# One run of row sums and value products per unit in a fused cross-attention kernel, with sums in a tile of their own and four input tile slots

## The chip, the cores and the metric

One core of a Trainium2 chip. The metric is the time of one execution in device microseconds. Engines: PE is TensorE's matmul, PEld its weight load, DVE is VectorE, ACT is ScalarE, POOL is GpSimd, SP issues transfers. Each engine runs its own instructions in the order written and waits on semaphores.

## What is computed

Cross-attention with 32 batches of 512 queries and 512 keys, width 512, 16 heads of 32, all in float32:

```python
qn, kvn = layer_norm(q, q_norm_g, q_norm_b), layer_norm(kv, kv_norm_g, kv_norm_b)
Q, K, V = heads(qn @ Wq), heads(kvn @ Wk), heads(kvn @ Wv)
attn = softmax(einsum('bhqd,bhkd->bhqk', Q, K) / sqrt(D_HEAD), axis=-1)
ctx = einsum('bhqk,bhkd->bhqd', attn, V)
out = q + gelu(ctx @ Wo + bo)        # exact gelu
```

## The kernel before

**Units and steps.** A batch is four steps, and step s works on several units at once. A unit is four heads of a batch: there are four in a batch, 128 in all. In step s of batch b TensorE computes, by names that the orders use:

- `q`, `k`: the query and key products of the unit two steps on, each 12 matmuls of 128x512 in six parts of two (three terms of high and low float32r parts by four chunks);
- `s`: 16 score matmuls of the next unit, from which VectorE takes the row maxima (`s` on its own list, L684);
- `m`: the transpose of these maxima. ScalarE (`mh`, L594) and VectorE (`ml`, L749) make a high and a low part of them, and four masked copies (`mx`, L598) put them into q_stack as extra rows, so that the transposed scores come out with the maximum subtracted;
- `st`: 16 transposed score matmuls of this unit. ScalarE takes the exponential of each into `probs` (L546, `st` on its list);
- `pv`: the value products of this unit, two for a unit (n = 0 and 1), each of two chunks by four heads. Each head's output is 32 partitions wide and the four stand side by side in `ctx_ps` (L864);
- `z`: the row sums of the preceding unit, a matmul by ones for each head, over chunks that GpSimd has added up (L876);
- `v`, `o`, `x`: value and output products (four tiles of six parts each per batch) and transposes of the eight normalised input tiles (four of x, four of the context) of the next batch.

A float32 matmul of the narrow kind is two records in the profile.

**Orders.** Who does what when is written out by hand in `ORDER`: a string for each step and engine. `s*3` is three of the next `s` of the step; kinds in `OVER_BATCH` and TensorE's v and o are counted over the batch. The steps of batches 1 to 30 are a loop on each engine; batches -1 (the head), 0, 31 and 32 (the tail) are unrolled with the parts that don't exist left out.

**Banks.** The transposed and plain scores rotate over four banks: score number i waits for the reader of i - 4 (`score_bank`, L332: an exponential or a maximum). Everything else but the values rotates over three banks `gen` in the order of first use (`gen_bank`, L317): a product waits until the one three before it is copied out. For q and k these are ScalarE's high part (L577, L589) and then VectorE's low part (L666), which frees the bank and lets SP restack the heads (`rq`, `rk`, L346).

**Normalising the unit.** Behind `z`, VectorE transposes the sums out of the bank (`zt`, L689, frees it), inverts (`zr`), spreads (`zb`) and multiplies `ctx_ps` by it (`cn`, L700, signals ctx_read); ScalarE and GpSimd split the result (`split`, L552, L490).

**Adding up.** GpSimd adds chunk c of `probs` into chunk c + 1 (`add`, L463, six a unit), once the values have been computed from both. The exponentials of the next unit wait for these additions, as they overwrite `probs`.

**Input tiles.** `tok` has eight slots, one for each tile of a batch. A load waits until the batch before has transposed its tile (L380). VectorE takes the statistics (`ln`, `la`, `lv`), GpSimd the deviation (`ln`), ScalarE normalises (`norm`), TensorE transposes (`x`), ScalarE and VectorE copy out (`x`).

**Biases.** `ob` adds the bias to an output tile in its bank (L725), `gelu` (L563) follows on ScalarE. Gelu and exponential need different activation tables; each change is a record of its own.

Of the kernel before, what the change touches and what calls it, by code (L numbers as in the profile page):

```python
# [5 lines left out]
ALU = mybir.AluOpType  # L6
# [54 lines left out]
    ),  # L61
    "act": (
# [4 lines left out]
    ),  # L67
    "dve": (
# [4 lines left out]
    ),  # L73
    "pool": (
        "ln*3 split add*6 res_add ln*3",
        "ln*2 add*5 res_add add res_add split res_add",
        "split add*6",
        "add split add*5",
    ),
    "sp": (  # L80
        "load*8 rq rk store res",
        "rq rk store res store",
        "store first_res rk rq first_res",
# [61 lines left out]
AFTER_ST = []  # L145
for _s in range(NU):
    _last = PLAN["pe"][_s].index(("st", NC - 1, HU - 1))
    AFTER_ST.append(next(_n for _kind, _n, _part in PLAN["pe"][_s][_last:] if _kind == "pv"))
# [7 lines left out]
for _s in range(NU):  # L156
    for _kind, _n, _part in PLAN["pe"][_s]:
        if _part == 0 and _kind in ("v", "o", "x"):
            GEN_AT[(_kind, _n)] = len(GEN)
            GEN.append((_kind, {"v": _s // (NU - 1), "o": -1, "x": 1}[_kind], _n, 2 * NC if _kind == "x" else NC))  # L160
        if _part == 0 and _kind in ("q", "k", "m", "z"):
            _off = _s + {"q": 2, "k": 2, "m": 1, "z": -1}[_kind]
            GEN_AT[(_kind, _off % NU)] = len(GEN)
            GEN.append((_kind, _off // NU, _off % NU, NU))
# [8 lines left out]
def build(nc, x, ctx_in, q_g, q_b, kv_g, kv_b, wq, wk, wv, wo, bo, out):  # L173
    B = x.shape[0]
    with ExitStack() as es:
# [17 lines left out]
        probs = sb("probs", [P, NC, HU, D])  # L193
        ctx_hl = sb("ctx_hl", [P, 2, NU, D], F32R)
        ctx_n = sb("ctx_n", [P, D])
        tok = sb("tok", [P, 2 * NC, D])
# [5 lines left out]
        ones = sb("ones", [P, P])  # L202
        maxes = sb("maxes", [P, 2, P])
        max_cut = sb("max_cut", [P, P], F32R)
        max_hl = sb("max_hl", [P, P], F32R)
        cut_sign = sb("cut_sign", [P, 1])
        low_row = sb("low_row", [P, 1])
# [9 lines left out]
        minus_half = sb("minus_half", [P, 1])  # L217
        bias_q = sb("bias_q", [P, NU])
        bias_k = sb("bias_k", [P, NU])
        bias_v = sb("bias_v", [P, NU])  # L220
        norm_rows = sb("norm_rows", [4 * NC, P])
# [36 lines left out]
        ln_shift = sem("ln_shift")  # L258
        z_inverted = sem("z_inverted")
# [113 lines left out]
        def _(sp):  # L373
# [583 lines left out]
```

## Time and profile before

| | us |
|---|---|
| median of two timed runs | 3285.81 (3284.95 to 3286.67) |
| the profiled execution, device time | 3289.35 |
| its span, first to last instruction | 3287.5 |
| PE busy in the span | 3251.8 (99%) |
| DVE, ACT, POOL busy | 2255.8, 2278.0, 2314.0 (69 to 70%) |
| PE, value products (L864) and row sums (L876) busy | 492.5 and 139.8 |

The mean granted TensorE clock is 0.995 of full speed. Matmuls are pipelined, and their ends in the profile are modelled: how long a run of them occupies the engine is read from the start of a row to the start of the next one, not from its own length. A row of the timeline merges instructions of one line; "x4" is their number, and what stands in brackets is idle time before it and who ended it.

### The profile page before, as it was taken

The page shows a single profiled execution, that of the slowest core. Times are in us where ns is not written, and L with a number is a line of the kernel's source. Part 1 is how long each engine was busy: PE and PEld are TensorE (multiplying, and loading weights), DVE is VectorE, ACT ScalarE, POOL GpSimd, SP SyncE. Part 2 cuts the span into 40 slices and gives each one's busy share as a digit, 9 for nine tenths or more (in the row PEclk, how much of TensorE's full clock was granted, in tenths as well). Part 3 has the DMA queues.
Part 4 walks back from the last instruction along what each step waited for, and adds up shares of the span by engine and source line. Part 5 has one row for each costly group of instructions (what it writes and reads, how often), then busy time and mean ns, then how long its engine had stood idle before and what let it go on. Part 6 is the DMA issues. An engine that isn't in the chain of part 4 may idle for free.

```text
span 3287.5 us, 60427 instructions
## 1 busy us (share of the span) xinstructions
PE 3251.8 (99%) x16611; PEld 2140.6 (65%) x16611; DVE 2255.8 (69%) x4775; ACT 2278.0 (69%) x3986; POOL 2314.0 (70%) x1543
## 2 busy tenths in 40 slices
PE   8999999999999999999999999999999999999998
PEld 5566666666666666666666666666666666666664
DVE  6677676776676676667766766766677667667664
ACT  4677767776667777677667667776776676677765
POOL 2677677777767776776777677767767766777765
PEclk9999999999999999999999999999999999999999
DMA  6566556566566666565665566665656655666653
GB/s 141 76 111 106 104 103 115 90 108 109 104 107 96 109 104 105 103 117 86 109 108 105 105 97 109 106 103 103 120 83 111 106 105 105 99 110 107 102 77 74
DMA packets 186492, 340.15 MB, mean 103 GB/s; under 512 B 20561, under 2 KB 20577, under 8 KB 186466
## 3 DMA queue, kind: packets, MB, share of 16 engines
q1 hardware_dynamic: 186000, 339.03, 60.0%
q10 hardware_dynamic: 466, 0.80, 0.2%
q8 instruction: 13, 0.21, 0.0%
q14 instruction: 13, 0.11, 0.0%
HBM read 104.87 MB, written 33.55 MB: 42 GB/s over the span
## 4 chain that ended last, share of the span: by engine, by line
PE 97%; DVE 1%; issue 1%; ACT 1%; DMA 0%; POOL 0%; SPq 0%; ACTq 0%; POOLq 0%; DVEq 0%
PE gen L820 42%; PE score L847 15%; PE score L840 15%; PE ctx L864 14%; PE gen L876 4%; PE gen L910 4%; PE gen L930 1%; DVE maxes L684 0%; POOL probs L463 0%; DMA k_stack<-k_nat 0%; PE score L766 0%; ACT q_stack L598 0%; PE ctx L795 0%; DVE stats L703 0%; PE gen L809 0%
## 5 line engine op out<-in xcount | busy, mean ns | idle before, releaser
L463 POOL TENSOR_TENSOR probs<-probs 128x1024 f32<-128x1024 f32 x762 | 1803.0, 2397 | 290.6 <-PE ctx L864 284.6
L684 DVE TENSOR_REDUCE maxes<-score 128x1 f32<-128x512 f32 x2048 | 1295.3, 681 | 199.9 <-PE score L847 199.0
L546 ACT ACTIVATE probs<-score 128x512 f32<-128x512 f32 x2048 | 1086.3, 620 | 141.3 <-PE score L840 136.2
L847 PE MATMUL score<-k_stack,q_stack 96*128 96x512 f32 x2048 | 761.2, 413 | 3.2 <-DVE maxes L684 2.2
L840 PE MATMUL score<-q_stack,k_stack 128*128 128x512 f32 x2048 | 698.1, 407 | 6.4 <-ACT q_stack L598 6.3
L847 PEld LDWEIGHTS score<-k_stack,q_stack 96*128 96x128 f32 x2048 | 378.5, 189 | 217.1 <-ACT probs L546 82.9
L840 PEld LDWEIGHTS score<-q_stack,k_stack 128*128 128x128 f32 x2048 | 374.1, 189 | 202.4 <-DVE maxes L684 58.2
L864 PE MATMUL ctx<-probs,v_sb 128*32 128x512 f32 x4096 | 492.5, 598 | 1.1 <-DVE ctx_n L700 1.1
L820 PE MATMUL gen<-w_v,cT 128*128 128x512 f32 x1536 | 462.2, 395 | 0.0
L820 PE MATMUL gen<-cT,w_k 128*128 128x512 f32 x1536 | 460.0, 398 | 0.2 <-DVE q_nat L666 0.2
L820 PE MATMUL gen<-xT,w_q 128*128 128x512 f32 x1536 | 450.5, 396 | 3.4 <-DVE w_q L622 0.4
L820 PE MATMUL gen<-w_o,ctx_hl 128*128 128x512 f32 x1488 | 416.9, 396 | 0.0
L479 POOL TENSOR_TENSOR rstd<-var_eps,minus_half 128x1 f32<-128x1 f32 x256 | 141.0, 551 | 354.6 <-DVE neg_mean L715 352.8
L490 POOL TENSOR_TENSOR ctx_hl<-ctx_n,ctx_hl 128x512 fp32r<-128x512 f32 x128 | 164.4, 1285 | 290.3 <-ACT ctx_hl L552 288.9
L598 ACT ACTIVATE q_stack<-max_hl,chunk_mask 32x512 fp32r<-32x512 f32 x512 | 326.2, 706 | 50.3 <-DVE max_hl L749 49.5
L820 PEld LDWEIGHTS gen<-w_v,cT 128*128 128x128 f32 x1536 | 287.6, 189 | 85.3 <-issue 26.0
L820 PEld LDWEIGHTS gen<-xT,w_q 128*128 128x128 f32 x1536 | 288.2, 189 | 69.9 <-issue 8.4
L820 PEld LDWEIGHTS gen<-cT,w_k 128*128 128x128 f32 x1536 | 286.7, 192 | 57.8 <-DVE q_nat L666 1.1
L666 DVE SCALAR_TENSOR_TENSOR k_nat<-gen,bias_k,k_nat 128x512 fp32r<-128x512 f32 x128 | 95.8, 749 | 325.1 <-ACT k_nat L589 325.1
L820 PEld LDWEIGHTS gen<-w_o,ctx_hl 128*128 128x128 f32 x1488 | 276.8, 189 | 57.3
L864 PEld LDWEIGHTS ctx<-probs,v_sb 128*32 128x32 f32 x4096 | 106.9, 109 | 237.3 <-issue 236.0
L666 DVE SCALAR_TENSOR_TENSOR q_nat<-gen,bias_q,q_nat 128x512 fp32r<-128x512 f32 x128 | 95.6, 747 | 231.4 <-ACT q_nat L577 231.4
(88 smaller groups left out, 2748.2 us busy)
## 6 DMA issues: line engine op xcount, KB each, us to landing
k_stack<-k_nat SPq DMA_DIRECT2D x384, 256.0 KB, 8.4
q_stack<-q_nat SPq DMA_DIRECT2D x381, 256.0 KB, 5.6
tok<-in_x SPq DMA_DIRECT2D x132, 256.0 KB, 10.4
tok<-in_ctx SPq DMA_DIRECT2D x128, 256.0 KB, 11.0
res<-in_x SPq DMA_DIRECT2D x124, 256.0 KB, 2.7
out<-res SPq DMA_DIRECT2D x124, 256.0 KB, 2.1
probs<-in_L_xattn_Wq SPq DMA_DIRECT2D x1, 1024.0 KB, 7.6
probs<-in_L_xattn_Wk SPq DMA_DIRECT2D x1, 1024.0 KB, 9.9
```

The lines of the kernel that those rows point to most:

```text
L463: pool.tensor_tensor(probs[:, c + 1, heads], probs[:, c + 1, heads], probs[:, c, heads], ALU.add).then_inc(pool_added, 1)
L479: pool.tensor_tensor(rstd[:, n:n + 1], var_eps[:, n:n + 1], minus_half[:], ALU.pow).then_inc(ln_rstd, 1)
L490: pool.tensor_tensor(ctx_hl[:, 1, up], ctx_n[:], raw(ctx_hl[:, 0, up]), ALU.subtract).then_inc(ctx_split, 1)
L546: act.activation(probs[:, n, part, :], score_at(s, "st", i)[:], ACT.Exp, scale=SCALE).then_inc(exp_done, 1)
L598: act.activation(q_stack[SROW:P, u1 % 2, :, P * n:P * (n + 1)], raw(max_hl[SROW:P, :]).unsqueeze(1).to_broadcast([SHIFTS, HU, P]), ACT.Ide ...
L666: dve.scalar_tensor_tensor(out=dst, in0=psum, scalar=bias, in1=raw(hi), op0=ALU.add, op1=ALU.subtract).then_inc(done, 1)
L684: dve.tensor_reduce(maxes[:, u1 % 2, SROW + i:SROW + i + 1], score_at(s, "s", i)[:], AX_X, ALU.max, negate=True).then_inc(max_done, 1)
L820: mm = pe.matmul(bank[:, :], stationary(hs, c), moving(hm, c), start=(i == 0), stop=(i == len(TERMS) * NC - 1))
L840: pe.matmul(score_bank(pe, b, s, "st", i)[:, :], k_stack[:, s % 2, part, P * n:P * (n + 1)], q_stack[:, s % 2, part, :], start=True, stop= ...
L847: pe.matmul(score_bank(pe, b, s, "s", i)[:, :], q_stack[0:KROWS, u1 % 2, n, P * part:P * (part + 1)], k_stack[0:KROWS, u1 % 2, n, :], star ...
L864: mm = pe.matmul(ctx_ps[DH * j:DH * (j + 1), :], v_sb[:, c, lo:lo + DH], probs[:, c, j, :], start=(c == 0), stop=(c == NC - 1))
L876: mm = pe.matmul(bank[DH * j:DH * (j + 1), :], ones[:, 0:DH], probs[:, c, j, :], start=(summed or c == 0), stop=(c == NC - 1))
```

## The change

- `z` is gone as an item of its own. `pv` is now once a unit and last among the products that need `probs`: the row sums of the preceding unit (4 matmuls, in a bank of `gen`) and right behind them all 16 value products of this unit (`values`).
- GpSimd's running sums go into a tile of their own, `sums`, instead of into `probs`. The first addition of a unit waits for the preceding unit's row sums (`full["z"]`). The exponentials wait for the additions that read their chunk and for the value products of the preceding unit.
- The values of a unit are copied out of `ctx_ps` by ScalarE into `ctx_raw` (`cc`, a new item, 128x512), which signals ctx_read and which the next value products wait for. Their normalising comes a step later: `zt` copies the sums out, `zb` writes the spread inverse back into the sums' bank, `cn` multiplies ctx_raw by it into ctx_n and only then frees the bank.
- `tok` has four slots. A load waits for the transpose of the tile four before.
- The orders of all engines are written anew.
- Small tiles are joined (max_hl into max_cut, three columns into row_consts, the three biases, norm_rows into max_cut, `ones` is 32 wide). The scaling of w_k in the head waits for all eight transposes, as its scratch is `tok`.

```diff
 ORDER = {
     "pe": (
-        "q*3 v q*2 v q v st*2 v*2 s st v s st s v*2 st s st s z v st*3 s v*2 st*2 s st k v s*4 pv st s st*2 o s "
-        "st s k s*2 pv m k o*2 k o k*2",
-        "o st*2 o st*3 q st q*4 st q st*3 z x k*3 x st*2 x st k*2 s k st s st*2 pv s x s x s x s pv s x s*2 o*3 "
-        "s*2 x o s o*2 s o s o*2 s o s o*3 m",
-        "o*4 s o s k s k s st k s st z st s st s q st q st s st*2 k st*3 k s st k st*4 pv s*2 q s q s*2 q s*2 q "
-        "pv m",
-        "k q k v q v k*2 st*3 k st*2 q st*2 k q st q st q st*2 z st*4 v st v s*3 pv s*2 v s*2 v s*2 v s v s*2 v*2 "
-        "s*2 v s*2 v pv m",
+        "q*6 v*2 st*4 v st v st v st*3 v st*2 v st*2 v st*2 v st s v s*2 v s*3 v s k s*2 pv s*4 k s k s k s k*2 m",
+        "q*6 x*2 st*4 x*2 st k*3 st k st*3 k st k st o st*2 o st*2 o st s o s*2 o s o pv s*2 x*3 s*4 o*4 s o s o "
+        "s o s o s o*2 s o*5 m o*3",
+        "x s*6 st*2 q st q st q st*2 q st*2 q st*2 q st*2 s st*3 s st s*4 pv s*4 k*5 m k",
+        "q*6 k st*4 k st*2 k st k st*2 k st*3 k st*2 v st*2 v*2 s*5 pv s*2 v s*2 v s v s v s*2 v s v s*2 v*3 m",
     ),
     "act": (
-        "q st*4 v st*8 norm v split norm*2 st*4 mh mx*4 k",
-        "st*6 gelu q st x st*2 norm st*4 x k st*2 norm x norm st x*2 norm x norm x*2 gelu mh gelu mx*4 split",
-        "gelu st*12 k split st*4 q mh mx*4",
-        "st*6 k st*5 q st*4 split st v*2 mh mx*4",
+        "q st*16 cc v norm*2 v norm*2 split k mh mx*4",
+        "q x*2 st x*2 st*15 k cc norm gelu norm*3 x*3 gelu*2 mh split x mx*4",
+        "gelu st*16 q cc split mh k mx*4",
+        "q st*16 k cc split v*2 mh mx*4",
     ),
     "dve": (
...
+        "q ln la ln la ln la ln la lv*4 s*9 zt zr zb cn s*7 md k ml",
+        "q x*4 ln la ln lv la ln lv la ln lv la lv s*2 ob s zt zr zb cn s k s*2 x*3 s*5 ob s*5 md ob ml",
+        "ob s*6 x s*3 q s*3 zt zr zb cn s*4 md ml k",
+        "q s*5 zt zr zb cn k s*11 md ml",
     ),
     "pool": (
...
+        "ln*4 add*6 split",
+        "ln*4 res_add add*4 res_add add res_add add split",
+        "res_add add*6 split",
+        "add*6 split",
     ),
     "sp": (
...
+        "load*4 rq rk",
+        "load*4 rq store rk",
+        "res store*2 first_res res store first_res rq rk",
         "rq rk",
     ),
 }
...
-                if valid(b - 1):
-                    wait(sp, full["x"], 8 * (b - 1) + i + 1)
+                if valid(b - 1) or i >= NC:
+                    wait(sp, full["x"], 8 * b + i - NC + 1)
...
                 wait(pool, exp_done, 16 * t + HU * (c + 1) + 2 * (half + 1))
-                wait(pool, pv_done, 4 * t + c + 2)
-                if c > 0:
+                if c == 0:
+                    wait(pool, full["z"], t)
+                else:
                     wait(pool, pool_added, 6 * t + n - 1)
...
+                before = probs[:, 0, heads] if c == 0 else sums[:, heads]
+                pool.tensor_tensor(sums[:, heads], probs[:, c + 1, heads], before, ALU.add).then_inc(pool_added, 1)
...
-                            if n < 3 and part % 2 == 0:
-                                wait(act, pool_added, 6 * (t - 1) + 2 * n + part // 2 + 1)
-                            if n == 3 and part == 0:
-                                wait(act, full["z"], t)
+                            if part % 2 == 0:
+                                wait(act, pool_added, 6 * (t - 1) + 2 * max(n - 1, 0) + part // 2 + 1)
+                            if part == 0:
+                                wait(act, pv_done, 4 * (t - 1) + n + 1)
...
+                        if kind == "cc" and valid(bp):
+                            wait(act, pv_done, 4 * (NU * bp + up) + 4)
+                            wait(act, free["z"], NU * bp + up)
+                            act.activation(ctx_raw[:], ctx_ps[:], ACT.Identity).then_inc(ctx_read, 1)
...
-                            dve.tensor_tensor(ctx_n[:], ctx_ps[:], ctx_n[:], ALU.mult).then_inc(ctx_read, 1)
+                            wait(dve, ctx_read, tp + 1)
+                            dve.tensor_tensor(ctx_n[:], ctx_raw[:], gen_at("z", up)[:], ALU.mult).then_inc(free["z"], 1)
...
+            def values(t, u):
+                wait(pe, exp_done, 16 * t + 16)
+                for c in range(NC):
+                    for j in range(HU):
+                        lo = P * u + DH * j
+                        mm = pe.matmul(ctx_ps[DH * j:DH * (j + 1), :], v_sb[:, c, lo:lo + DH], probs[:, c, j, :],
+                                       start=(c == 0), stop=(c == NC - 1))
+                        if c == 0 and j == 0:
+                            mm.then_inc(stack_used, 1)
+                    mm.then_inc(pv_done, 1)
...
+                        if kind == "pv" and valid(bp):
+                            bank = gen_bank(pe, b, "z", up)
+                            at_end = last(bp) and up == NU - 1
...
+                            else:
+                                wait(pe, pool_added, 6 * tp + 6)
+                            for c in range(NC if at_end else 1):
...
+                        if kind == "pv" and valid(b):
+                            wait(pe, ctx_read, t)
+                            if s == 0:
+                                wait(pe, free["v"], 4 * b + 4)
+                            values(t, s)
```

## Rows read from the trace of the kernel before

**Rows 1.** The page: the span, and the chain that ended last by engine.

```profile
span 3287.5 us, 60427 instructions
...
PE 97%; DVE 1%; issue 1%; ACT 1%; DMA 0%; POOL 0%; SPq 0%; ACTq 0%; POOLq 0%; DVEq 0%
```

**Rows 2.** Sums by stretch, one batch: length, busy us by engine, clock, DMA share, GB/s.

```profile
core 0: us, PE busy (x) PEld busy (x) DVE busy (x) ACT busy (x) POOL busy (x), PEclk, DMA share, GB/s
1671.98:1772.32 100.34, 100.27 (x516) 66.34 (x517) 69.81 (x148) 70.78 (x125) 72.57 (x49) 1.00 0.61 105
```

**Rows 3.** Timeline of PE around row sums and values: start, length, instruction.

```profile
1680.82 0.39 PE L847 MATMUL score<-k_stack,q_stack 96*128 96x512 f32 x1
1681.14 1.07 PE L876 MATMUL gen<-probs,ones 128*32 128x512 f32 x8
1682.14 0.73 PE L820 MATMUL gen<-w_v,cT 128*128 128x512 f32 x2
1682.71 0.86 PE L840 MATMUL score<-q_stack,k_stack 128*128 128x512 f32 x3
...
1687.42 1.92 PE L864 MATMUL ctx<-probs,v_sb 128*32 128x512 f32 x16
1689.28 0.50 PE L840 MATMUL score<-q_stack,k_stack 128*128 128x512 f32 x1
```

**Rows 4.** Timeline of PE, the transposed maxima between output products.

```profile
1726.66 0.30 PE L930 MATMUL gen<-ident,maxes 128*128 128x128 f32 x1
1726.72 2.07 PE L820 MATMUL gen<-w_o,ctx_hl 128*128 128x512 f32 x8
1728.63 0.40 PE L847 MATMUL score<-k_stack,q_stack 96*128 96x512 f32 x1
```

**Rows 5.** Timelines of PE, ACT, DVE: a query product's last pair and its copies.

```profile
1675.28 0.61 PE L820 MATMUL gen<-xT,w_q 128*128 128x512 f32 x2
1676.02 0.69 ACT L577 ACTIVATE q_nat<-gen,bias_q 128x512 fp32r<-128x512 f32 x1 [0.65 <-PE gen L820]
1676.74 0.75 DVE L666 SCALAR_TENSOR_TENSOR q_nat<-gen,bias_q,q_nat 128x512 fp32r<-128x512 f32 x1 [3.96 <-ACT q_nat L577]
```

**Rows 6.** Timelines of PE and ACT: a tile's transposes and its first copy.

```profile
1720.38 0.60 PE L910 MATMUL gen<-ident,tok 128*128 128x128 f32 x4
1721.02 0.60 ACT L571 ACTIVATE cT<-gen 128x512 fp32r<-128x512 f32 x1 [2.15 <-PE gen L910]
```

**Rows 7.** Timeline of ACT: exponentials, masked copies, gelu, table load, exponentials.

```profile
1698.86 3.03 ACT L546 ACTIVATE probs<-score 128x512 f32<-128x512 f32 x6
...
1728.01 2.55 ACT L598 ACTIVATE q_stack<-max_hl,chunk_mask 32x512 fp32r<-32x512 f32 x4
...
1731.12 0.58 ACT L563 ACTIVATE act_out<-gen 128x512 f32<-128x512 f32 x1
1731.72 1.28 ACT L546 ACT_TABLE_LOAD   x1
1733.01 2.07 ACT L546 ACTIVATE probs<-score 128x512 f32<-128x512 f32 x4
```

**Rows 8.** Timeline of PE in the tail: maxima's transpose, then transposed scores.

```profile
3250.20 0.30 PE L930 MATMUL gen<-ident,maxes 128*128 128x128 f32 x1 [0.34 <-DVE maxes L743]
3253.92 4.98 PE L840 MATMUL score<-q_stack,k_stack 128*128 128x512 f32 x11 [3.42 <-ACT q_stack L598]
```

**Rows 9.** Timeline of DVE: from the sums' transpose to the next work; thirteen maxima.

```profile
1758.05 0.72 DVE L689 STREAM_TRANSPOSE ctx_n<-gen 128x512 f32<-128x512 f32 x1 [1.48 <-PE gen L876]
...
1760.53 0.74 DVE L666 SCALAR_TENSOR_TENSOR q_nat<-gen,bias_q,q_nat 128x512 fp32r<-128x512 f32 x1
...
1763.62 7.86 DVE L684 TENSOR_REDUCE maxes<-score 128x1 f32<-128x512 f32 x13 [0.56 <-PE score L847]
```

**Rows 10.** Timeline of POOL: the six additions of a unit.

```profile
1742.19 14.24 POOL L463 TENSOR_TENSOR probs<-probs 128x1024 f32<-128x1024 f32 x6
```

**Rows 11.** Timeline of ACT in the head: the scaling of w_k.

```profile
21.50 4.11 ACT L519 ACTIVATE tok<-probs,norm_cols 128x512 f32<-128x512 f32 x4
```

**Rows 12.** DMA issues: the last weight, KB each, median us to landing.

```profile
probs<-in_L_xattn_Wo SPq DMA_DIRECT2D x1, 1024.0 KB, 14.5
```

More of the change, by code:

```diff
@@ L160 @@
             GEN.append((_kind, {"v": _s // (NU - 1), "o": -1, "x": 1}[_kind], _n, 2 * NC if _kind == "x" else NC))
[L161 to L164, printed above, removed]
+        if _part == 0 and (_kind in ("q", "k", "m") or _kind == "pv"):
+            _off = _s + {"q": 2, "k": 2, "m": 1, "pv": -1}[_kind]
+            _unit = "z" if _kind == "pv" else _kind
+            GEN_AT[(_unit, _off % NU)] = len(GEN)
+            GEN.append((_unit, _off // NU, _off % NU, NU))
 def bank_before(i, count, banks):
@@ L216, in build @@
         rstd = sb("rstd", [P, 8])
[L217 to L221, printed above, removed]
+        bias_qkv = sb("bias_qkv", [P, 3, NU])
+        bias_q, bias_k, bias_v = (bias_qkv[:, n, :] for n in range(3))
         norm_cols = sb("norm_cols", [P, 4, NC])
@@ L258, in build @@
         ln_shift = sem("ln_shift")
+        z_turned = sem("z_turned")
         z_inverted = sem("z_inverted")
@@ L759, in _ @@
             pe.wait_ge(cols_loaded, 16 * 4)
-            pe.matmul(score[3][:, 0:4 * NC], norm_rows[:], ident[0:4 * NC, 0:4 * NC], start=True, stop=True,
+            pe.matmul(score[3][:, 0:4 * NC], raw(max_cut[0:4 * NC, :]), ident[0:4 * NC, 0:4 * NC], start=True, stop=True,
                       is_transpose=True).then_inc(cols_mm, 1)
@@ L848, in batch @@
                                       k_stack[0:KROWS, u1 % 2, n, :], start=True, stop=True).then_inc(s_full, 1)
-                        if (kind, n) == ("pv", 1) and last(b) and s == NU - 1:
-                            wait(pe, ctx_split, NU * B - 2)
-                            for kind2, count in (("z", NU * B - 1), ("m", NU * B), ("q", NU * B), ("k", NU * B),
-                                                 ("x", 2 * NC * B), ("v", NC * B), ("o", NC * (B - 1))):
-                                wait(pe, free[kind2], count)
-                            last_products((0, 1), (0, 1))
@@ L869, in batch @@
-                        if kind == "z" and valid(bp):
-                            bank = gen_bank(pe, b, "z", up)
-                            summed = not (last(bp) and up == NU - 1)
-                            if summed:
-                                wait(pe, pool_added, 6 * tp + 6)
-                            for c in (NC - 1,) if summed else range(NC):
-                                for j in range(HU):
-                                    mm = pe.matmul(bank[DH * j:DH * (j + 1), :], ones[:, 0:DH], probs[:, c, j, :],
-                                                   start=(summed or c == 0), stop=(c == NC - 1))
+                        if kind == "pv" and valid(bp):
+                            bank = gen_bank(pe, b, "z", up)
+                            at_end = last(bp) and up == NU - 1
+                            if at_end:
+                                wait(pe, ctx_split, NU * B - 2)
+                                for kind2, count in (("z", NU * B - 1), ("m", NU * B), ("q", NU * B), ("k", NU * B),
+                                                     ("x", 2 * NC * B), ("v", NC * B), ("o", NC * (B - 1))):
+                                    wait(pe, free[kind2], count)
+                            else:
+                                wait(pe, pool_added, 6 * tp + 6)
+                            for c in range(NC if at_end else 1):
+                                for j in range(HU):
+                                    mm = pe.matmul(bank[DH * j:DH * (j + 1), :], ones[:, 0:DH],
+                                                   probs[:, c, j, :] if at_end else sums[:, j, :], start=(c == 0),
+                                                   stop=(not at_end or c == NC - 1))
```

87 lines of the change are left out of this document (32 added, 55 removed), and 4 rows, old and new, of the table ORDER.

## The prediction, made before the change was run

> **What bounds the kernel now.** I read the chain of work that ended last first. TensorE holds 97% of it, and nearly all of the 3287.5 us span is one instruction of TensorE after another [rows 1]. Then the sums by stretch: one batch of the loop takes 100.34 us with TensorE busy for 100.27, while VectorE and ScalarE are busy for 70 and 71 and GpSimd for 73 [rows 2]. So only what TensorE's own stream costs counts, until one of the others makes it wait. 128 units in 32 batches of four steps: a microsecond per batch is 32 us in the end. The profiled execution took 3289.35 us on the device's clock, 3.5 above the median of the two timed runs.
>
> The last view is TensorE in order of time around the narrow products (outputs of 32 partitions, four side by side). A row's start minus the start of the next is what a run costs. A product part is two matmuls in 0.455, a score 0.23. The score ahead of the row sums starts 0.32 before them instead of 0.23; the sums (8 records) occupy 1.00, the values (16 records) 1.86; the pair that follows takes 0.57 in place of 0.455 [rows 3]. Two unknowns from two runs: 8 records more cost 0.86, so a run is 0.14 plus 0.107 a record, and each run costs 0.09 ahead and 0.11 behind on top. **A run of narrow products costs 0.34 us whatever its length.**
>
> The Trainium skill, "TensorEngine Tiling (Array Packing)", Key Properties, says that changing the tiling mode drains the engine, switching tiles within it does not. The trace agrees (the 0.34), and by this rule alone the change would only gain; that is the first rival.
>
> **The change, part by part, for one batch.**
>
> *Runs.* Before: three runs a unit, twelve a batch. After: one a unit, four in all, 40 records each, 0.14 + 4.28 = 4.43 us. Eight runs less at 0.34: **-2.7 us**. If switching from the sums' bank to the values' costs a run's start again, 4 x 0.34 = 1.4 of this is lost; if all old runs had also hidden a wait, nothing more is gained. I take 2.7, as bank and weights change inside a values run already.
>
> *Transposes.* The transposed maxima (m) stood behind a values run in three units; now all four stand alone, which costs 0.06 to the next start and 0.09 in the eight products after it [rows 4]: 3 x 0.11 = +0.3 at most, 0 at least. The eight input tiles (x) go in four groups instead of seven: -0.2. Old small waits, 0.3 to 0.5, vanish or stay. **If TensorE never waited, a batch would last 100.34 - 2.7 + 0.3 - 0.2 - 0.4 = 97.3 us.**
>
> *What the new order makes TensorE wait for.* I walk the four steps with 0.455 a product part, 0.23 a score, 0.44 a tile, 4.43 + 0.2 a run, and put beside it the queues of the other engines, which run strictly in the order written. Four places come out late.
>
> (A) End of step 0 is k*2 m, then q*6. The three work banks rotate in order of first use: k, sums, m, q, so this q takes k's bank and must wait for k's copies. From a product's last pair to ScalarE's copy is 0.74, to VectorE's low part 0.72 more, which takes 0.75 [rows 5]: 2.2 us. TensorE has 0.455 + 0.1 of work until then, and VectorE's seven maxima and md behind the sums' chain end at about the same time. **+1.5** (1.2 to 1.7).
>
> (B) Step 2 begins x s*6 st*2. ScalarE's queue reads, from the end of step 1, x, four masked copies (mx), gelu, and then 16 exponentials, q, the new copy cc. Its x cannot start before TensorE has transposed the tile with which step 2 begins: 0.64 after its start [rows 6]. Then 0.48 for the copy, 2.45 for mx, 0.60 for gelu, 1.29 for the table load before the first exponential [rows 7]: first exponential at 5.5. They follow each other at 0.48 to 0.49 [rows 7]: the sixteenth is done at 5.5 + 15 x 0.48 + 0.62 = 13.3. The last of the s*4 takes its bank, so the run starts at 13.6. TensorE's work up to there is one x, 12 + 16 scores and 6 parts: 0.44 + 6.4 + 2.7 + 0.2 = 9.8. **+3.8.** Before, the first values run of a unit needed eight exponentials only, and this step had the last o products in front. Bounds: 2.5 if ScalarE gets its gelu and load done before mx by luck of order (its queue forbids it), 4.5 with the copies q and cc (another 1.15) not hidden behind the sums' 0.9.
>
> The Trainium skill, "ScalarE: Activation LUTs", What ACT_TABLE_LOAD costs, gives 1283 ns for a load plus about 1380 of drain, 2.66 in all for a switch. The trace has 1.28 and the exponential 0.01 behind it; by the page (B) would be 5.2 instead of 3.8, an estimate that I don't use.
>
> (C) Beginning of step 3. From m to the first st in the tail, where nothing else stands between, is 3.72 [rows 8]; the order has m k, q*6 k = 3.7, but k's copy (0.57) goes ahead of mx. The exponentials then run at their own pace. **+0.4** (0 to 0.9, the top if k's restack, issued behind a late k, lands after the first s).
>
> (D) End of step 3. VectorE has s*5, the sums' chain and k, then s*11 and md. From the transpose of the sums to the instruction behind the chain is 2.48 [rows 9]; k is 0.66, thirteen maxima take 7.86, so eleven 6.6 [rows 9]. The five end at 14.2 from the step's start: 14.2 + 2.5 + 0.7 + 6.6 + 0.2 = 24.2, where TensorE comes to m at 23.4. **+0.8** (0 to 1.0).
>
> Priced at nothing: the new cc copies (4 x 0.5 on ScalarE) lie behind the last exponentials under the sums' head in steps 0, 1 and 3, and are 0.9 late at most. GpSimd's additions, 14.2 for six [rows 10], now begin only behind the row sums of the preceding unit, at about 15.7 of step 0 whose length is 24.8: they end 5 us into the next, where the ninth exponential (needs the fourth) is at 8 or later; in step 1 three res_add and a gelu at 17 push them 3 us, and they still end 3 us into step 2. With that cover gone each microsecond would come out on exponentials. Four tile slots: the loads of c tiles wait for x transposes of step 1 (at 3 to 6 us), land by 9, and are normalised by 12; their transposes are at 19.6. Two table loads less a batch, 2.6 on ScalarE, are off the path.
>
> Sum: 97.3 + 1.5 + 3.8 + 0.4 + 0.8 = 103.8, **+3.5 us a batch**, 32 x 3.5 = 111. The head adds about 5: c tiles are now queued behind the weights, the last of which lands 14.5 after its issue [rows 12], and the scaling of w_k, at 21.5 before [rows 11], waits for all eight tiles (0 to 8). Tail: 0, within 3. 3289.35 + 116 = 3405 in a profiled execution, **3402 us** against the median.
>
> **The rivals.**
> 1. *Only the runs count* (the other side): planned waits are hidden, as they are in the kernel before, whose order keeps TensorE busy for 100.27 of 100.34 us [rows 2]. 97.3 a batch: 3286 - 97 + 5 = 3194. For it: the 2.7 is sure. It needs (A) and (B) both to be wrong; it decides as soon as all waits are under 3.0 us a batch. Chance 0.10.
> 2. *Half of the waits.* (B) is 1.5 and (A) or (D) vanish, because ScalarE reaches mx before the x copy matters: 100.8 a batch, 3286 + 15 + 5 = 3306, no measurable change. Against it: ScalarE's queue. 0.18.
> 3. *Main forecast*, 3350 to 3440: 0.60.
> 4. *More waits than I see*: cc and q not hidden, k's restack late, or additions late on the exponentials, +1.5 a batch: 3450. 0.12.
> That the change doesn't do what it says (a wait between sums and values that splits the run) is in 4: +11.
>
> **The numbers.** Likeliest 3402; range 3310 to 3445 leaves out rival 1, half of rival 4 and the low edge of rival 2. 2% is 66 us, about what a measurement of this kernel can tell from no change: faster 0.10, same 0.18, slower 0.72.
>
> **What would show it.** In the changed profile: one run of 40 records, 4.4 us, per unit; a batch of 103.8; TensorE's idle time in step 2, ahead of the scores and of the run, released by ScalarE's exponentials and its masked copies (3.8 a batch, 120 us in all); product q of step 1 released by VectorE's k_nat (1.5, 48 in all); m released by VectorE (0.8). A batch of 97 to 98 with TensorE at 99% refutes me; one where run and sums are split by a wait shows ctx_read late. I am wrong if ScalarE runs its exponentials of step 2 before 4 us after that step's x.

## The result, and the profile after

| kernel | us, median (runs) | ratio to the kernel before, 95% interval |
|---|---|---|
| before | 3285.81 (3284.95 to 3286.67) | |
| changed | 3499.55 (3498.73 to 3500.37) | 1.065 (1.0605 to 1.0696) |

The change makes the kernel 6.5% slower. The direction and the places were forecast, the size was not: +214 us instead of +116, and outside the range.

The page of the changed kernel: its span, TensorE's busy time, and the chain of work that ended last, by engine.

```profile
span 3496.9 us, 60533 instructions
...
PE 74%; DVE 12%; issue 7%; ACT 6%; DVEq 0%; DMA 0%; ACTq 0%; POOL 0%
```

The chain was 97% TensorE before [rows 1]; now a quarter of it lies on the other engines. One batch and its four steps (length, busy us by engine, clock, DMA share, GB/s), to be held against [rows 2]:

```profile
1673.21:1779.69 106.48, 102.47 (x516) 66.63 (x517) 71.20 (x148) 69.99 (x127) 72.25 (x49) 1.00 0.57 98
1673.21:1698.41 25.20, 23.94 (x121) 15.83 (x122) 17.75 (x44) 17.07 (x32) 15.93 (x15) 1.00 0.46 83
1698.41:1731.14 32.73, 32.71 (x174) 23.54 (x175) 24.26 (x55) 22.25 (x40) 23.59 (x20) 1.00 0.74 128
1731.14:1754.13 22.99, 21.28 (x102) 11.50 (x101) 14.46 (x24) 15.66 (x28) 13.38 (x8) 1.00 0.40 91
1754.13:1779.69 25.56, 24.55 (x122) 15.76 (x121) 14.74 (x25) 15.00 (x29) 19.35 (x9) 1.00 0.62 82
```

A batch takes 106.5 instead of 100.34, and the work of the other engines is what it was. TensorE's idle time is 4.0 of the 6.1 us; the rest hides in its "busy" time, as the next section shows. TensorE's waits (who waits for whom: us in total, times, longest):

```profile
PE score L851 <- ACT q_stack L598: 54.5, 63, 3.4
PE gen L933 <- DVE maxes L743: 52.2, 66, 2.2
PE gen L913 <- ACT tok L567: 11.7, 2, 6.4
PE gen L831 <- DVE k_nat L666: 10.2, 32, 0.3
```

Before, the first two were 6.3 us in 3 waits and 3.9 in 3. In order of time, TensorE at the end of step 0, the run of step 1, and step 2 (start, length, instruction, idle time before):

```profile
1696.23 0.62 PE L831 MATMUL gen<-cT,w_k 128*128 128x512 f32 x2
1697.79 0.30 PE L933 MATMUL gen<-ident,maxes 128*128 128x128 f32 x1 [0.94 <-DVE maxes L743]
1698.41 1.45 PE L831 MATMUL gen<-xT,w_q 128*128 128x512 f32 x5 [0.32 <-DVE k_nat L666]
...
1713.84 1.07 PE L872 MATMUL gen<-sums,ones 128*32 128x512 f32 x8
1714.72 3.62 PE L810 MATMUL ctx<-probs,v_sb 128*32 128x512 f32 x32
1718.27 0.73 PE L858 MATMUL score<-k_stack,q_stack 96*128 96x512 f32 x2
...
1731.14 0.60 PE L913 MATMUL gen<-ident,tok 128*128 128x128 f32 x4
1731.49 1.17 PE L858 MATMUL score<-k_stack,q_stack 96*128 96x512 f32 x4
1732.81 1.10 PE L858 MATMUL score<-k_stack,q_stack 96*128 96x512 f32 x2 [0.15 <-DVE maxes L684]
1735.35 0.73 PE L851 MATMUL score<-q_stack,k_stack 128*128 128x512 f32 x2 [1.44 <-ACT q_stack L598]
...
1745.58 1.07 PE L872 MATMUL gen<-sums,ones 128*32 128x512 f32 x8
```

The run does what the change says: 40 records one behind the other, 1718.27 - 1713.84 = 4.43 us, the length forecast from [rows 3]. The price is in front of it. ScalarE in step 2, the same stretch:

```profile
1731.40 0.63 ACT L552 ACTIVATE ctx_hl<-ctx_n 128x512 fp32r<-128x512 f32 x1 [0.76 <-PE gen L831]
1732.05 0.60 ACT L571 ACTIVATE cT<-gen 128x512 fp32r<-128x512 f32 x1
1732.68 2.54 ACT L598 ACTIVATE q_stack<-max_cut,chunk_mask 32x512 fp32r<-32x512 f32 x4
1735.24 0.60 ACT L563 ACTIVATE act_out<-gen 128x512 f32<-128x512 f32 x1
1735.86 1.28 ACT L542 ACT_TABLE_LOAD   x1
1737.15 7.94 ACT L542 ACTIVATE probs<-score 128x512 f32<-128x512 f32 x16
1745.12 0.69 ACT L577 ACTIVATE q_nat<-gen,bias_qkv 128x512 fp32r<-128x512 f32 x1
```

It is the chain (B) of the prediction, link for link: copy, four masked copies, gelu, load, sixteen exponentials, and the run 0.49 us behind the last of them.

**An account of TensorE's time.** For what follows I sort every distance between the starts of two successive TensorE instructions over 24 or 26 batches of a trace by its neighbours. Undisturbed, a product or score is followed by the next after 0.23; 0.105 more for the first one behind a narrow run and 0.085 behind transposes; 0.33 lead into a narrow run and 0.52 out of its last group. What a distance has above that is "excess": waits, the slow first instruction behind a wait, the pace of an engine that TensorE follows, and a lowered clock.

| kernel | a batch | undisturbed | excess |
|---|---|---|---|
| before | 100.4 | 97.4 | 3.0 |
| changed | 106.9 | 95.3 | 11.6 |

The split between the two columns is good to some 0.4: if a distance is sorted by the instruction two before and by its place within a run as well, the undisturbed sums are 97.6 and 95.1 and the excess 2.8 and 11.7. So the merged runs and the grouped transposes do bring 2.1 us a batch (2.5 by the finer sorting), and disturbances take 8.6 (9.0). The total, in the profiled executions, 3498.73 - 3289.35 = 209.4: 197.3 in the 31 batches between the same places of both streams, 8.5 ahead of them and 3.6 behind.

### The profile page after: what moved, and what is told of

Its sections match the earlier page's. It is cut to its first block, busy times and chain, and to the rows that moved or that the text cites. A ratio compares the mean times of both kernels' runs of the same rounds, so it can differ in the third digit from the quotient of the medians.

```text
span 3496.9 us, 60533 instructions
## 1 busy us (share of the span) xinstructions
PE 3333.0 (95%) x16611; PEld 2177.4 (62%) x16611; DVE 2297.7 (66%) x4775; ACT 2257.8 (65%) x4052; POOL 2301.7 (66%) x1543
## 4 chain that ended last, share of the span: by engine, by line
PE 74%; DVE 12%; issue 7%; ACT 6%; DVEq 0%; DMA 0%; ACTq 0%; POOL 0%
PE gen L831 32%; PE score L851 16%; PE ctx L810 9%; PE score L858 9%; DVE maxes L684 8%; ACT q_stack L598 4%; PE gen L913 3%; PE gen L872 3%; DVE k_nat L666 1%; DVE gen L695 1%; PE gen L933 1%; DVE ctx_n L689 1%; ACT ctx_hl L552 1%; ACT k_nat L589 0%; DVE maxes L743 0%
## 5 line engine op out<-in xcount | busy, mean ns | idle before, releaser
L460 POOL TENSOR_TENSOR sums<-probs,sums 128x1024 f32<-128x1024 f32 x508 | 1198.9, 2386 | 0.0
L542 ACT ACTIVATE probs<-score 128x512 f32<-128x512 f32 x2048 | 1024.7, 673 | 19.2 <-PE score L851 17.1
L460 POOL TENSOR_TENSOR sums<-probs 128x1024 f32<-128x1024 f32 x254 | 599.4, 2381 | 589.4 <-PE gen L872 589.4
L851 PE MATMUL score<-q_stack,k_stack 128*128 128x512 f32 x2048 | 720.6, 424 | 56.3 <-ACT q_stack L598 54.5
L858 PE MATMUL score<-k_stack,q_stack 96*128 96x512 f32 x2048 | 717.3, 419 | 11.1 <-DVE maxes L684 4.1
L810 PE MATMUL ctx<-probs,v_sb 128*32 128x512 f32 x4096 | 463.0, 593 | 1.0 <-ACT ctx_raw L547 1.0
L831 PE MATMUL gen<-xT,w_q 128*128 128x512 f32 x1536 | 427.2, 412 | 16.9 <-DVE k_nat L666 10.2
L475 POOL TENSOR_TENSOR rstd<-var_eps,row_consts 128x1 f32<-128x1 f32 x256 | 140.6, 549 | 350.3 <-DVE neg_mean L715 344.8
L598 ACT ACTIVATE q_stack<-max_cut,chunk_mask 32x512 fp32r<-32x512 f32 x512 | 326.1, 705 | 34.8 <-DVE max_cut L749 33.2
L552 ACT ACTIVATE ctx_hl<-ctx_n 128x512 fp32r<-128x512 f32 x128 | 81.0, 633 | 401.0 <-DVE ctx_n L700 376.9
L810 PEld LDWEIGHTS ctx<-probs,v_sb 128*32 128x32 f32 x4096 | 132.9, 110 | 307.3 <-issue 276.9
L666 DVE SCALAR_TENSOR_TENSOR q_nat<-gen,bias_qkv,q_nat 128x512 fp32r<-128x512 f32 x128 | 96.1, 751 | 311.6 <-ACT q_nat L577 311.6
```

Source lines behind the costliest of these rows:

```text
L460: pool.tensor_tensor(sums[:, heads], probs[:, c + 1, heads], before, ALU.add).then_inc(pool_added, 1)
L475: pool.tensor_tensor(rstd[:, n:n + 1], var_eps[:, n:n + 1], minus_half, ALU.pow).then_inc(ln_rstd, 1)
L542: act.activation(probs[:, n, part, :], score_at(s, "st", i)[:], ACT.Exp, scale=SCALE).then_inc(exp_done, 1)
L552: act.activation(ctx_hl[:, 0, up, :], ctx_n[:], ACT.Identity).then_inc(ctx_hi, 1)
L598: act.activation(q_stack[SROW:P, u1 % 2, :, P * n:P * (n + 1)], raw(max_cut[SROW:P, :]).unsqueeze(1).to_broadcast([SHIFTS, HU, P]), ACT.Id ...
L666: dve.scalar_tensor_tensor(out=dst, in0=psum, scalar=bias, in1=raw(hi), op0=ALU.add, op1=ALU.subtract).then_inc(done, 1)
```

## The experiments

Each time is the median of its runs, beside runs of the kernel before on the same chip (3286.7 to 3286.9); each ratio is to these, with its 95% interval. Where the text speaks of batches at full clock, it means those of the 30 loop batches in whose stretch the trace shows no granted clock below 1.00 (see the last section).

**1. The table load of step 2.** One function in the changed kernel:

```diff
-    act.activation(dst, o_bank(b - 1, n)[:], ACT.Gelu)
+    act.activation(dst, o_bank(b - 1, n)[:], ACT.Identity)
```

> The changed kernel with its gelus computed as plain copies (Identity), so that ScalarE never changes its table; the output is not the reference's. All else as in the changed kernel, gelus included as instructions. Theory (waits): in step 2 the exponentials start behind x, four masked copies, gelu and a table load of 1.28, and the run of narrow products starts behind the sixteenth; without the load the run starts 1.28 earlier, so x to run falls from 14.4 to about 13.1 and a batch from 106.7 to 105.4: 32 x 1.3 = 41 us, 3458 against 3499.5. If a load also cost a drain behind it, as the Trainium skill (ScalarE: Activation LUTs, What ACT_TABLE_LOAD costs) has it, twice as much, 3415. Rival 1: the run of step 2 is held by something else (the additions, TensorE's own work, a reduced clock): no change, 3495 to 3500.

Measured: 3466.44 us, 33 less than the changed kernel (ratio 1.0552, 1.0534 to 1.057). ScalarE, then TensorE's last tile and its run, in one step 2:

```profile
1826.63 0.60 ACT L563 ACTIVATE act_out<-gen 128x512 f32<-128x512 f32 x1
1827.27 8.37 ACT L542 ACTIVATE probs<-score 128x512 f32<-128x512 f32 x16
...
1822.53 0.60 PE L913 MATMUL gen<-ident,tok 128*128 128x128 f32 x4
...
1836.12 1.07 PE L872 MATMUL gen<-sums,ones 128*32 128x512 f32 x8
```

The exponentials start 0.04 behind the gelu instead of 1.31, and tile to run is 13.59 instead of 14.44. The chain holds, but only 0.85 of the 1.28 comes back in this step: the sixteen exponentials now last 8.37 instead of 7.94, since they begin before TensorE, which itself waited for the masked copies, has scores for them. Batches at full clock are 0.88 shorter than the changed kernel's (28 us over all); the other 5 us come from the clock, which fell in 6 batches of 30 instead of 18. A load took 1.28 and the next exponential started 0.01 behind it. The Trainium skill ("ScalarE: Activation LUTs", What ACT_TABLE_LOAD costs) counts about 1380 ns of drain to the load's 1283; neither this trace nor the 33 us (85 were expected by it) shows that drain on the path here.

**2 and 3. Cheaper readers of the scores, in both kernels.**

```diff
-    act.activation(probs[:, n, part, :], score_at(s, "st", i)[:], ACT.Exp,
+    act.activation(probs[:, n, part, 0:D // 2], score_at(s, "st", i)[:, 0:D // 2], ACT.Exp,
                    scale=SCALE).then_inc(exp_done, 1)
...
-    dve.tensor_reduce(maxes[:, u1 % 2, SROW + i:SROW + i + 1], score_at(s, "s", i)[:], AX_X, ALU.max,
+    dve.tensor_reduce(maxes[:, u1 % 2, SROW + i:SROW + i + 1], score_at(s, "s", i)[:, 0:D // 2], AX_X, ALU.max,
```

> The changed kernel, its maxima and its exponentials over 256 of the 512 columns each (the output is not the reference's): VectorE and ScalarE have about 0.27 and 0.2 less per score tile, TensorE's work is unchanged. Theory (waits): the exponentials' pace, the late maxima ahead of m and the restart costs behind them go; what stays is product q of step 1 on k's bank (1.5) and in step 2 the four masked copies (1.6 ahead of the first st). 97.3 + 1.5 + 1.6 + 0.4 = 100.8 a batch, 31 x 5.9 = 183 less: 3315 (3290 to 3340). Rival 1 (the loss is in TensorE itself: a long run costs more than its parts, or its clock is reduced): still 3450 or more. Rival 2 (GpSimd's additions, unchanged here, hold the exponentials): 3400 or more, with TensorE's waits released by exponentials as before.

> The kernel before, with the same cut of its maxima and exponentials to 256 columns (the output is not the reference's). TensorE is busy for 100.27 of 100.35 us, so nearly nothing is to be had: its small waits, 0.3 to 0.5 a batch, go: 99.9 a batch, 3272 (3265 to 3283). Together with the changed kernel under the same cut this gives what the change does to TensorE's stream alone: theory, (100.8 - 3.1 of waits left) - 99.9 = -2.2 a batch. Rival (small waits are many more than seen): under 3260.

Measured: changed kernel 3355.29 (ratio 1.0207, 1.019 to 1.0225), kernel before 3253.82 (0.9899, 0.9882 to 0.9915). The cut takes 144 us from the changed kernel and 33 from the one before; 102 us of the 214 stay. Both lie outside their ranges, by expectations 1.3 and 0.6 us a batch off: the changed kernel keeps more, the kernel before had more to give. Still, a kernel whose runs themselves had cost the time would have stayed at 3450 or more. TensorE's waits in the changed kernel under the cut:

```profile
PE score L851 <- ACT q_stack L598: 69.5, 61, 3.4
PE gen L831 <- DVE k_nat L666: 43.9, 32, 1.4
PE gen L831 <- ACT v_sb L557: 20.8, 32, 0.7
```

The late maxima are gone, and behind them stands what they hid: product q of step 1 on k's bank (1.37 a batch, 1.5 forecast in (A)) and at the end of step 3 v's bank (0.65), which I had not seen. By the account: 102.4 a batch, of which the excess at these two places is 2.5, in step 2 ahead of the first st 2.2, at the start of step 3 0.4. Without these four (less the 0.36 that the loop's edge costs in both kernels) 97.7 a batch remain, where the prediction had 97.3 for a TensorE that never waits; the kernel before takes 99.4 under the same cut, so the change is worth -1.7 to TensorE's stream where nothing late is in its way, for -2.2 expected.

**4 and 5. VectorE or ScalarE.** The two halves of that edit, each alone, in the changed kernel.

> The changed kernel with its maxima alone over 256 columns (the output is not the reference's): VectorE's share of the waits. The waits on late maxima ahead of m (52 us in all) go, but behind them stand k's bank (1.4) and at the end of step 3 v's (0.7), which the kernel with both cuts showed, so little is gained: -0.5 a batch, 3483 (3470 to 3492). Rival (VectorE's lateness is what the change costs): -2 a batch or more, 3435 and under.

> The changed kernel with its exponentials alone over 256 columns (the output is not the reference's): ScalarE's share. In step 2 the sixteenth exponential ends before TensorE reaches the run; what stays of that step's wait is the part ahead of the first st, which the masked copies release (2.2). -1.7 a batch by pace, and -0.3 to -0.6 if the stretches at the lower of TensorE's two clocks, which follow the wait in step 2, go as they did without the table load: 3435 (3420 to 3450). Rival: the same as with both cuts, 3355, if VectorE's part is nothing; 3490 if ScalarE's is.

Measured: 3461.71 with cheap maxima (38 less), 3441.64 with cheap exponentials (58 less). Together they had brought 144, 48 more than the sum of the two. Most of that difference is TensorE's clock. With cheap exponentials alone it fell in 24 of the 30 loop batches. One such batch and the next, at full clock (length, busy us by engine, clock, DMA share, GB/s):

```profile
1753.51:1858.96 105.45, 101.36 (x517) 68.76 (x517) 71.18 (x148) 59.56 (x127) 72.32 (x49) 0.98 0.58 99
1858.96:1962.79 103.83, 99.69 (x516) 67.62 (x517) 71.16 (x148) 59.22 (x127) 72.32 (x49) 1.00 0.59 101
```

With cheap maxima alone it fell in 29 of 30 (105.8 a batch, the one other 105.3). Batches at full clock take 106.4 in the changed kernel, 105.3 with cheap maxima (that one batch), 103.85 with cheap exponentials and 102.4 with both: 1.2, 2.6 and 4.1 us less. So neither engine is "the" cause; ScalarE's pace weighs about two thirds and VectorE's one third, and hardly anything needs both. My 3483 for the first was too high: step 3 lost 1.0 of excess, more than the v bank gives back.

**6. The price of a run by itself.** Under both cuts, the row sums get a token of their own ("rs"), one score ahead of the values' run, in all four steps (in step 1 a product stands between them too):

```diff
-  "... s*2 o s o pv s*2 x*3 s*4 o*4 ...",
+  "... s*2 o rs s o pv s*2 x*3 s*4 o*4 ...",
```

> The changed kernel with maxima and exponentials over 256 columns, and in addition the row sums taken out of the values' run: one score stands between them in each of the four steps, so there are eight runs of narrow products a batch instead of four, with the same products. Theory: a run costs 0.34 whatever its length, and nothing waits near it under this cut: 4 x 0.34 = +1.36 a batch, +43 us on the kernel with the cut alone (35 to 52). Rival 1 (a run costs less, the 0.34 held hidden waits of the kernel before): +10 to +25. Rival 2 (the entry is hidden by loading weights): 0.

Measured: 3452.59 us (ratio 1.0506, 1.0489 to 1.0524), 97 more than without the split. TensorE around the two runs of a unit:

```profile
1827.67 0.94 PE L858 MATMUL score<-k_stack,q_stack 96*128 96x512 f32 x3
1828.54 1.07 PE L872 MATMUL gen<-sums,ones 128*32 128x512 f32 x8
1829.54 0.51 PE L858 MATMUL score<-k_stack,q_stack 96*128 96x512 f32 x1
1829.97 3.64 PE L810 MATMUL ctx<-probs,v_sb 128*32 128x512 f32 x32
1833.55 1.20 PE L858 MATMUL score<-k_stack,q_stack 96*128 96x512 f32 x4
```

Sums to score 1.00, score to values 0.43, values to score 3.58: 5.01, less 0.23 for the score, 4.78 against 4.43 for the single run: 0.35 a run, as forecast, of which 0.1 is the lone score's own, between two runs. The same comparison gives 0.34 to 0.35 in the other three steps: 1.4 a batch or 44 us, where 43 was forecast. The other 53 are not the run's price: the order of the work banks changed with the new token, so that a transpose of step 1 now waits for k's bank (0.5 a batch, 16 us by the difference of that distance), and TensorE's clock fell in 29 of the 30 loop batches. These take 105.7, the one other 104.1; that is about 44 us more than the kernel without the split loses by its clock. (The three add up to a little more than 97; the head is 3 us shorter.) One stretch of 3.4 us behind the wait of step 2, first of this kernel, then the same place without the split (length, busy us by engine, clock, DMA share, GB/s):

```profile
1819.40:1822.80 3.40, 3.40 (x10) 2.67 (x10) 0.00 (x0) 2.59 (x5) 1.28 (x1) 0.61 0.33 126
```

```profile
1771.40:1774.80 3.40, 3.40 (x16) 2.79 (x16) 0.00 (x0) 3.12 (x8) 1.32 (x2) 1.00 0.42 145
```

Ten instructions instead of sixteen in the same time, at a granted clock of 0.61 instead of 1.00; both come right behind a wait of 1.98 us on the masked copies.

**7. One part of the change alone.** The kernel before, the two halves of the values in one run in steps 1, 2 and 3 (row sums apart, as they were):

```diff
-  "... s st*2 pv s x s x s x s pv s x s*2 o*3 ..."
+  "... s st*2 s x s x s x s pv*2 s x s*2 o*3 ..."
-  "... k st*4 pv s*2 q s q s*2 q s*2 q pv m",
+  "... k st*4 s*2 q pv*2 s q s*2 q s*2 q m",
-  "... s*3 pv s*2 v s*2 v s*2 v s v s*2 v*2 s*2 v s*2 v pv m",
+  "... s*3 pv*2 s*2 v s*2 v s*2 v s v s*2 v*2 s*2 v s*2 v m",
```

> The kernel before, with one part of the change alone: the two halves of a unit's values in one run, in steps 1, 2 and 3 (in step 0 they stay as they were), row sums where they were and still added up inside the probabilities. Three runs of narrow products fewer a batch. Theory (a joined run postpones what is queued behind it): GpSimd may add chunk 1 into chunk 0's place only behind the values that read it, so its six additions of 14.2 us start 1 to 5 us later, and the next unit's exponentials, which write over what is added, wait for them; a walk of the queues with the durations of the rows gives +7 us a batch: 3500 (3460 to 3530), with TensorE's waits released by ScalarE's exponentials. Rival (only the runs count, 0.34 each): 3 x 0.34 = -1.0 a batch, 3254.

Measured: 3568.48 us (ratio 1.0856, 1.0838 to 1.0874), the slowest kernel of the study, with three runs fewer a batch. The sign was right, the size short, and the reason wrong: no row of ScalarE's waits names the additions. TensorE's waits, then VectorE's largest one on scores, in this kernel:

```profile
PE gen L930 <- DVE maxes L743: 97.4, 65, 2.2
PE score L847 <- ACT probs L546: 57.9, 65, 1.1
PE score L847 <- DMA k_stack<-k_nat: 19.1, 31, 3.2
...
DVE maxes L684 <- PE score L847: 420.3, 330, 3.7
```

and VectorE's in the kernel before:

```profile
DVE maxes L684 <- PE score L847: 199.0, 239, 3.3
```

VectorE first stands idle for want of scores (420 us instead of 199), and then TensorE waits for its last maxima (97 us instead of 4). A joined run is 3.6 us without a single score, and four score banks hold what VectorE and ScalarE work off sooner than that; what they miss there they make up at the end, ahead of m. In two of the three steps moreover the second half had stood right before m and had covered VectorE's last maxima. Some 42 of the 282 us are the clock's: 29 of 30 loop batches have a slow stretch, here in step 0, and take 109.3 against 107.8 of the one that has none.

**8. The same with cheaper readers.**

> The kernel before with its values joined in steps 1, 2 and 3, and besides its maxima and exponentials over 256 columns (the output is not the reference's). Joining alone cost 282 us; the additions, which I had blamed, show no wait of an exponential there. New theory (a run of narrow products makes no scores: while it lasts, 3.6 instead of 1.9 us, VectorE and ScalarE empty the four score banks and stand idle, and VectorE's maxima then end late, ahead of m): with cheaper maxima and exponentials they catch up sooner, and about half of the loss stays, 140 us on the 3254 of the kernel before under the same cut: 3395 (3350 to 3440). Rival 1 (GpSimd's additions, untouched by the cut): the loss stays whole, 3536. Rival 2 (no wait is left, only three runs fewer): 3254 - 33 = 3221.

Measured: 3402.59 us (ratio 1.0352, 1.0336 to 1.0368), 149 above the kernel before under the same cut (3253.82), where joining had cost 282. The new theory expected about 140, the additions 282. So 133 us hang on the readers of the scores, some 42 of them by way of the clock, which doesn't fall in any loop batch here. The cut also ends the exponentials earlier, for which the additions wait, so this run alone would not clear GpSimd; ScalarE's waits in run 7 do. The other 149 us stay. TensorE's waits here are on late maxima (30.0 us), on exponentials (23.1), on k's restack (21.4) and on the masked copies (16.7); how the rest divides was not tried.

**9 to 11. Other orders.** I wrote a walk of all the queues, with the durations of the traces, and let it look for orders. First for the changed kernel (only the table differs; its core, as an example):

```diff
-  "x s*6 st*2 q st q st q st*2 q st*2 q st*2 q st*2 s st*3 s st s*4 pv s*4 k*5 m k",
+  "s*6 st q s st*2 q st s st q st s st q st s st*3 s st q st*2 s st q st s*2 pv s k s k*4 m k",
```

> The changed kernel with the same work in other orders: the last x tile leaves step 2 for the end of step 1, ScalarE's split of step 3 moves behind its masked copies, scores s and st are mixed in all steps so that maxima and exponentials find work earlier. The computation is the reference's. Theory (the waits come from the order, not from the merged run): step 2's wait falls from 5 to 1.5 and step 0's end from 1.1 to 0.3; a walk of the queues gives 3.6 a batch less than the changed kernel, and the stretches at the lower clock should go: 3375 (3345 to 3400), still above the kernel before. Rival (merged runs can't be had without these waits): 3450 or more.

Measured: 3428.02 (ratio 1.0428, 1.0411 to 1.0445): 72 less than the changed kernel, 53 above my figure. The walk had transfers too fast: here VectorE waits 108 us for input tiles, and the copy of the context comes late in step 2 and splits the run (0.66 a batch between sums and values, the case that the prediction priced at 11 us in all). With a slower transfer and longer hand-offs in the walk, a search again, from both kernels:

> The changed kernel with a second set of orders, made as in e11 by a walk that now has the transfers at the slower rate that e9 showed (there VectorE waited for tile loads and the run was split by the copy of the context). The computation is the reference's. Theory: 3.4 us a batch less than the changed kernel and no stretch at the lower clock: 3499 - 109 - 10 = 3380 (3350 to 3410), so that the merged run still loses against the kernel before, because four late places of TensorE (end of step 0, step 2's start, end of step 3, the x tiles of step 1) can't all be covered. Rival (the merged run is free once the order is right): under 3290.

> The kernel before, its code and its three runs of narrow products a unit untouched, with other orders in its table, found by a walk of the queues with the durations that the traces show (waits and a slower transfer rate included, after what e9 showed): in step 0 all but two of the o products leave for step 1, x tiles stand in pairs, scores of both kinds and the products are mixed so that each of the four score banks is emptied in time. The computation is the reference's. Theory: before's 3.0 us a batch of small waits and mode changes falls by 1.3: 3286 - 42 = 3244 (3225 to 3280). Rival (the walk doesn't see what binds, as in e9, where it was 50 us too low): 3290 to 3340.

Measured: the changed kernel in the second set of orders 3371.21 (ratio 1.0257, 1.0241 to 1.0272), 128 us less than the changed kernel and within 9 of the figure; the kernel before in new orders 3302.34 (1.0048, 1.0034 to 1.0062), 16 more instead of 42 less. So 60% of the change's loss was its order. TensorE's waits in the first of them:

```profile
PE gen L932 <- DVE maxes L742: 40.3, 66, 3.4
PE gen L912 <- ACT tok L566: 12.2, 2, 7.4
PE score L850 <- ACT q_stack L597: 11.4, 32, 3.4
PE gen L912 <- DVE q_nat L665: 9.5, 31, 0.3
```

The wait on the masked copies fell from 54.5 to 11.4 and the clock stayed up, but the maxima ahead of m are still late (40.3). No version of the merged run that I found beats the kernel before, and the walk, good to 1 or 2 us a batch, is no guide for gains as small as those left in it.

## Why the prediction was right or wrong

All by batch, from the account of TensorE's distances.

- **Runs: right.** 4.43 us for 40 records was exact; 0.34 a run is 0.34 to 0.35 in the split kernel.
- **Undisturbed stream: -2.1 instead of -2.6** (the eight runs, m's and x's together), or -2.5 by the finer sorting: right, as far as the account can tell.
- **Old small waits: mis-sized.** I put them at 0.3 to 0.5, to be had by the change. The kernel before has 3.0 us of excess a batch, nearly all of it inside "busy": PE showed 100.27 of 100.34 busy [rows 2], but a first instruction behind a wait is 0.1 longer, and scores that follow their reader's pace count as busy too. The cut to half columns got 1.0 of it back. The changed kernel has about 3.2 outside the four places, so nothing of this vanished: +0.65 against my sum.
- **(A) end of step 0: right.** 1.10 ahead of m and 0.55 ahead of q, 1.65 for 1.5; without the late maxima k's bank alone costs it, as walked.
- **(B) step 2: the mechanism right, the size short, 5.4 for 3.8.** This is the step that failed most. In batches at full clock the run starts 14.44 behind the tile's transposes instead of 13.6, and TensorE's own work up to there is 9.6 and not 9.8: a wait of 4.8. The first exponential came at 6.0, not 5.5. ScalarE's copy of the tile started 0.91 behind the transposes and not 0.64 [rows 6], because the split of the preceding context (ctx_hl, L552), which stands ahead of it in the queue, came only 0.76 late; and the prediction had put the copy at 0.48 and the masked copies at 2.45, where [rows 6] and [rows 7] show 0.60 and 2.55 (here 0.63 and 2.56 to the next instruction). The sixteenth exponential ends at 13.95 instead of 13.3, and the run starts 0.49 behind it and not 0.3, since three scores and their banks lie between. TensorE's own scores in this stretch follow the exponentials with 0.1 to 0.26 of excess each; that is how this wait is spent, and no further term. Then the clock: in the batches where it fell behind the wait, 18 of 30, tile to run took 14.8 to 15.2, which makes another 0.4 on average. The last 0.2 lie behind the run.
- **A lowered clock: not in the sum at all.** See the last section; about 12 us of 214, contained in (B).
- **(C) 0.5 for 0.4, (D) 0.8 for 0.8: right.**
- **Head 8.5 for 5, tail 3.6 for 0**: short by 7 us in all. TensorE waits 11.7 for normalised tiles in the head, 3.5 before.
- **Zero prices.** The additions held: ScalarE has no wait on them worth a row. The cc copies and the four tile slots show in none of TensorE's waits in the changed kernel, though VectorE already waits 42 us there for tiles of c (none before); the slots and the cc copy bind as soon as the order is tightened (run 9). The two table loads fewer were not tried by themselves.

The sum, then: +1.9 at the four places (of which the clock 0.4), +0.65 for small waits that stayed, +0.5 for the stream (by the finer sorting 0.1, and 0.4 more of small waits): 3.0 a batch above the 3.5 forecast, 6.5 in all. The first rival (only the runs count) is refuted twice, by the changed kernel and by run 7; the fourth (more waits than I see, 3450) was nearest, yet not by its mechanisms: neither q nor cc nor k's restack was it. How the 8.6 us of excess divide between engines is known for the 4.1 that the two halves of the cut remove (runs 4 and 5); for the rest, the masked copies and the banks of k and v, it stays open.

## What to carry to other kernels

Merging short runs saves a fixed price each (0.34 us here), and what decides is the other side: during a run that feeds nobody, the engines that read TensorE's results stand idle, and with only four banks between them they can't work ahead; on engines that are 70% busy, that time is missed at the next point where TensorE needs their last result. So before lengthening a run, compare its length with the work that the banks hold, and look at what stands between the last score and its consumer. And where TensorE is "99% busy", compare starts with the undisturbed distance: 3% of this kernel was excess that the profile counts as work.

## What the runs showed that I had not expected

**A lower clock behind a wait.** In step 2 of the changed kernel 18 of the 30 loop batches go on at half pace after the wait. Two stretches of one such batch, behind the wait and a little later (columns as above):

```profile
1841.80:1845.20 3.40, 3.37 (x9) 2.56 (x10) 1.03 (x2) 3.37 (x6) 1.21 (x2) 0.64 0.44 154
1845.60:1849.00 3.40, 3.40 (x15) 2.68 (x14) 0.00 (x0) 2.78 (x7) 0.27 (x1) 0.92 0.20 77
```

Products there start every 0.427 us instead of 0.23, the lower of the clock's two levels (1.2 and 2.4 GHz), for about 3.4 us. Loop batches with such a stretch: none in the kernel before, 6 without the table load, 2 with both cuts, 29 with cheap maxima and 24 with cheap exponentials alone, 29 with the sums apart, 29 in the kernel with joined values (there in step 0), 3 and none in the changed kernel's two reordered versions. What a stretch costs is read from batches with and without it in one trace: 107.1 against 106.4 in the changed kernel, 0.66 each or 12 us in all, since part of it is hidden behind a later wait. With cheap exponentials it is 105.4 against 103.85, 37 us. The kernels with both cuts and with the sums apart have the same 1.98 us wait at this place, one at full clock in 28 of 30 batches, the other with a slow stretch in 29; so the wait alone doesn't decide it. What else decides was not found.

**Waits behind waits.** v's bank at the end of step 3 cost 20.8 us that no row of the changed kernel shows: it only appears once the late maxima in front of it are gone, as k's bank grows from 10.2 to 43.9.
